# Two layers of gated cross-attention with feed-forward: batch 0's keys and queries copied to the stacks directly, queries stored once in rows of 1,600 bytes, scatters placed beside the value projection

## The reference

```python
# x: (16, 100, 256), ctx_1024: (16, 361, 256), mask: (16, 1, 100, 361)
q = split_heads(queries @ Wq + bq)
k = split_heads(keys @ Wk + bk)
v = split_heads(values @ Wv + bv)
scores = jnp.einsum('bhqd,bhkd->bhqk', q, k) / jnp.sqrt(jnp.float32(HD))
scores = jnp.where(mask, jnp.float32(-1000000000000000.0), scores)
attn = jax.nn.softmax(scores, axis=-1)
...
x = x + jnp.tanh(g_xattn[0]) * _L0_xattn_ref(_layernorm(x, axis=-1), ctx_1024, ctx_1024, mask, ...)
x = x + jnp.tanh(g_ffn[0]) * _L0_ffn_ref(_layernorm(x, axis=-1), ...)     # top 2 of 8 experts, and a shared one
x = x + jnp.tanh(g_xattn[1]) * _L1_xattn_ref(_layernorm(x, axis=-1), ctx_1024, ...)
x = x + jnp.tanh(g_ffn[1]) * _L1_ffn_ref(_layernorm(x, axis=-1), ...)     # top 1 of 8, low-rank additions
```

## Time and profile before

| | us |
|---|---|
| median of 3 runs | 911.53 |
| lowest and highest | 909.79, 912.62 |
| the profiled execution | 903.28 |
| its span | 901.4 |
| its mean granted TensorE clock | 0.951 |

### The profile page before, as it was taken

How to read it: one execution, slowest core, us unless ns; L and a number is a source line. 1 busy time by engine, 2 the same in 40 slices (tenths; PEclk the granted TensorE clock), 3 DMA queues, 4 the chain that set the end, 5 groups by cost and what they waited for, 6 DMA issues and landing times.

```text
span 901.4 us, 22259 instructions
## 1 busy us (share of the span) xinstructions
PE 794.3 (88%) x7992; PEld 614.1 (68%) x7992; DVE 582.5 (65%) x1773; ACT 471.0 (52%) x1004; POOL 221.3 (25%) x213
## 2 busy tenths in 40 slices
PE   5579999998999987899997689889999999778996
PEld 3346777766676665578985467667677676557996
DVE  4867778776666665675546478778788777463332
ACT  2335556555455545645663156556566565535453
POOL 2535222233332314410007253224212111000000
PEclk9789999999999999999999679999999999879999
DMA  6966778776676741733324958878898875000001
GB/s 186 236 155 163 165 148 176 160 156 139 144 164 148 164 107 34 216 94 107 123 86 112 180 127 173 198 186 176 189 192 161 181 159 97 2 1 1 19 19 37
DMA packets 152379, 119.00 MB, mean 132 GB/s; under 512 B 81020, under 2 KB 143848, under 8 KB 152264
## 3 DMA queue, kind: packets, MB, share of 16 engines
q1 hardware_dynamic: 146656, 109.91, 54.6%
q0 software_dynamic: 4096, 6.57, 2.8%
q10 hardware_dynamic: 1520, 1.12, 0.5%
HBM read 77.84 MB, written 39.46 MB: 130 GB/s over the span
## 4 chain that ended last, share of the span: by engine, by line
PE 61%; DMA 12%; DVE 10%; issue 7%; SPq 5%; ACT 3%; POOL 1%; DVEq 0%; ACTq 0%; POOLq 0%
PE ps L1895 18%; PE ps L2008 8%; PE ps L2034 7%; PE ps L2067 6%; PE ps L2057 5%; DMA cT<-in_ctxT 5%; PE ps L2053 3%; DMA QS<-mp 3%; DMA scr_q<-qp 2%; PE ps L2091 2%; PE ps L2322 2%; DMA QS<-scr_q 2%; DVE mx L1523 2%; DVE ps L1519 2%; SPq L409 1%
## 5 line engine op out<-in xcount | busy, mean ns | idle before, releaser
L965 ACT ACTIVATE prob<-ps 128x400 f32<-128x400 f32 (+1 forms) x384 | 182.6, 500 | 95.9 <-PE ps L2057 88.5
L2034 PE MATMUL ps<-KS,QS 96*100 96x361 bf16 x512 | 168.0, 344 | 24.4 <-DVE mx L1519 9.7
L1519 DVE CUSTOM_DVE_ANT_0 ps<-ps,biasq 100x361 f32<-100x361 f32 x256 | 135.7, 542 | 72.7 <-PE ps L2034 68.9
L1523 DVE TENSOR_REDUCE mx<-ps 100x1 f32<-100x361 f32 x256 | 127.1, 527 | 55.1 <-PE ps L2034 52.5
L2057 PEld LDWEIGHTS ps<-QS,KS 98*128 98x128 bf16 x1536 | 110.2, 101 | 50.8 <-issue 11.2
L2057 PE MATMUL ps<-QS,KS 98*128 98x100 bf16 x1536 | 134.8, 212 | 6.2 <-ACT prob L965 4.5
L2008 PE MATMUL ps<-cT,wk 128*128 128x361 f32 x256 | 103.0, 514 | 16.5 <-DMA ident<-in_ident 9.3
L2034 PEld LDWEIGHTS ps<-KS,QS 96*100 96x100 bf16 x512 | 65.1, 128 | 62.0 <-DVE mx L1519 16.2
L2067 PE MATMUL ps<-prob,V 128*17 128x100 f32 (+1 forms) x3072 | 88.4, 255 | 11.8 <-issue 11.8
L702 POOL TENSOR_TENSOR kp<-kr,kp 128x722 bf16<-128x722 f32 x32 | 48.5, 1517 | 187.2 <-ACT kp L936 187.0
L2067 PEld LDWEIGHTS ps<-prob,V 128*17 128x17 f32 (+1 forms) x3072 | 67.7, 99 | 29.7 <-issue 26.5
(11 more groups left out here) (226 smaller groups left out, 1621.1 us busy)
## 6 DMA issues: line engine op xcount, KB each, us to landing
scr_k<-kp SPq DMA_DIRECT2D x96, 180.5 KB, 5.1
KS<-scr_k SPq DMA_DIRECT2D x64, 270.8 KB
cT<-in_ctxT SPq DMA_DIRECT2D x32, 361.0 KB, 4.5
KS<-scr_k SPq DMA_DIRECT2D x64, 180.5 KB
QS<-scr_q SPq DMA_DIRECT2D x64, 150.0 KB
KS<-scr_k SPq DMA_DIRECT2D x64, 90.2 KB
scr_q<-qp SPq DMA_DIRECT2D x24, 200.0 KB, 3.6
scr_q<-qp SPq DMA_DIRECT2D x48, 100.0 KB, 5.1
```

Of the source, the lines that this page charges most:

```text
L965: nc.scalar.activation(prob[0:KROWS[t], t, hg, :], ps[0:KROWS[t], c % 2, 0:HQ * S], ACT.Exp).then_inc(a["exp"], 1)
L1519: nc.vector.tensor_tensor_reduce(ps[0:S, banks[h % len(banks)], 0:S2], ps[0:S, banks[h % len(banks)], 0:S2], biasq[p][:, :], 1.0, -3.0e38, ...
L1523: nc.vector.reduce_max(mx[:, h:h + 1], ps[0:S, banks[h % len(banks)], 0:S2], axis=AX.X).then_inc(a["max"], 1)
L2034: mm(ps[0:S, banks[h % len(banks)], 0:S2], QS[p][0:SROWS, h, :], KS[p][0:SROWS, h * S2:(h + 1) * S2], start=True, stop=True).then_inc(a["s ...
```

## The change

**Batch 0.** In both layers its keys and queries go from `kp` and `qp` straight into KS[0] and QS[0] by DMA, 12 copies of 16 partitions x 8 heads each for keys, 12 for queries, in halves. The two halves of queries have semaphores of their own. For this the columns of the projection weights are ordered by half, then dimension, then head. `k_first` of batch 1 now waits until batch 0's keys have been copied, and that of batch 2 until the stores of batch 1 have landed.

**Query stores and loads.** Each piece is stored once, in two halves, six DMAs in all. A load of half a batch is three DMAs, whose source is repeated by a zero stride where a piece is needed three times or twice; a row is 8 heads x 100 columns = 1,600 bytes.

**Scatters.** One for each of the steps n = 8 to 11, two for each of 12 to 15, twelve in all; they wait for `pv`, the end of the burst. Twenty follow behind the last burst: three, the norm of the last pair, five, the two low pieces, twelve.

**The rest.** The rows of ones come from a small memset through `scr_ones` in DRAM; the memsets of V stand at the program's start; SP loads the small vectors first; layer 1's last weights are loaded in steps 8 to 13 (before, 2 to 10); in both prologues TensorE, ScalarE, VectorE and GpSimd have another order, with the first maxima ahead of the norm that stood before them.

```diff
+        SCATTERS = {8: (0,), 9: (1,), 10: (2,), 11: (3,), 12: (4, 5), 13: (6, 7), 14: (8, 9), 15: (10, 11)}
...
+            def first_keys(l, part, halves):
...
+                for half in halves:
+                    c = slice(half * HH * S2, (half + 1) * HH * S2)
+                    for r in range(NST):
+                        if KPART[r] == part:
+                            sp.dma_start(KS[0][r * HD:(r + 1) * HD, c], kp[:, part, half, :]).then_inc(sd["kload"][half][0], 16)
+
+            def first_queries(l, half):
+
+                for r in range(NST):
+                    queries_split(l, 0, QPART[r])
+                    sp.dma_start(QS[0][r * HD:(r + 1) * HD, half * HH:(half + 1) * HH, :],
+                                 qp[0][:, QPART[r], half, 0:S]).then_inc(s_fq[half], 16)
...
-                sp.dma_start(QS[p][0:SROWS, hs, :],
-                             scr_q[:, :, :, bass.ds(n * S, S)].rearrange("j k (d h) n -> (j k d) h n", h=H)[:, hs]).then_inc(sd["kload"][half][p], 16)
+                for part, (r, copies) in enumerate(QRUNS):
+                    rows = scr_q[half, part, n].rearrange("(d h) n -> d (h n)", h=HH)
+                    sp.dma_start(QS[p][r * HD:(r + copies) * HD, half * HH:(half + 1) * HH, :],
+                                 bc(rows.unsqueeze(0), [copies, HD, HH * S])).then_inc(sd["kload"][half][p], 16)
...
-                for r in range(NST):
...
-                    sp.dma_start(scr_q[r, :, :, g * GT:(g + 1) * GT].rearrange("k p n -> p k n"),
-                                 qp[u][:, QPART[r], :, :]).then_inc(q["stored"], 16)
+                for part in range(NPIECE):
+                    queries_split(l, g, part)
+                    for half in range(KT):
+                        sp.dma_start(scr_q[half, part, g * nb + t0:(g + 1) * nb].rearrange("t p n -> p t n"),
+                                     qp[u][:, part, half, t0 * S:nb * S].rearrange("p (t n) -> p t n", n=S)).then_inc(q["stored"], 16)
...
-                    nc.gpsimd.memset(KS[1][SROWS:KSROWS, :], 1.0).then_inc(s_vones, 1)
...
                         if n >= 8:
-                            pool.wait_ge(sa[0]["sT"], START + 3 * NHG * (n - 1))
-                            scatter(n - 8)
+                            pool.wait_ge(sa[0]["pv"], START + NHG * n)
+                            for i in SCATTERS[n]:
+                                scatter(i // 2, i % 2)
...
+            for i in range(12, 15):
+                scatter(i // 2, i % 2)
             norm_pair(F0, NPAIR - 1)
...
+            for i in range(15, 20):
+                scatter(i // 2, i % 2)
             for j in POOL_PIECES:
                 low_piece(j)
+            for i in range(20, 2 * B):
+                scatter(i // 2, i % 2)
```

394 lines of the change are left out of this document (202 added, 192 removed).

## The result

The changed kernel takes 969.14 us (median of 4 runs, 960.96 to 978.24) against 912.08 for the kernel before in the same comparison. One of the four, the 978.24, was a slow execution, and the ratio leaves it out: 1.059, its 95% interval 1.050 to 1.068. The forecast was a gain of 2%. The range, 870 to 928, does not hold the time, and the sign is wrong. The profiled run of the changed kernel took 971.69 us, its span 969.8, with a mean granted clock of 0.914 in place of 0.951.

What follows compares the result with a forecast made beforehand. TensorE, busy for 88% of the span, was taken as the limit, savings lying in its pauses, lowered clock and slower instructions. Terms -18 - 5 + 7 - 10 - 7 + 4 + 10 = -19: 884 us profiled, 892 median, range 870 to 928.

Steps and rivals of the forecast that it cites:

- steady steps: query stores and loads: Steps of both layers: more load issues in SP's queue, less a saved wait; +4 in layer 0, +10 in layer 1.
- The 3.9 us taken off for smaller stores: Layer 1's steps: halved query store bytes can remove the 3.9 us wait for the query stack.
- rival B: Steps of both layers: query loads fill two or three DMA engines and slow every step; 937 us, chance 0.19.
- Prologue of layer 0: Start of layer 0: direct copies give earlier scores, and VectorE's pause of 6.46 us goes; -10 us, bounds -6 and -13.
- Prologue of layer 1: Start of layer 1: direct copies take away the 4.28 us wait for the query stack; -7 us (-3 to -11).
- Rival C: Both prologues: they don't shorten, batch 1's stack arriving late, and give 3 of 17 us; 906 us, chance 0.10.
- Scatters: Layer 0's steps: scatters moved behind the burst no longer stall TensorE; -18 us, bounds -20 and -7.
- rival A: Layer 0's steps: scatters behind the burst hold ScalarE, then TensorE, so stalls move; 901 us, chance 0.15.
- Behind step 14: Layer 0 after step 14: four scatters issued later no longer hold ScalarE's copy and TensorE; -5 us (-3 to -6).
- The later slot rows: After layer 0's steps: last scatters come later, slot rows turn 6.5 us late, TensorE restarts below its clock; +7 (0 to +9).
- The wait that I named as its mark: Before the slot rows are turned: a wait of about 5 us would show the price of later scatters.

Runs made afterwards that it cites:

- The rung for them: Changed kernel with the query stores and loads of before, each half's load in three DMAs, source not repeated: 908.02 us, ratio 1.033.
- the first comparison: Here: kernel before with only the scatters moved, twelve in the steps after the burst, twenty behind them: 887.17 us, 0.987 against the kernel before at 898.12.
- the third: Here: kernel before with its scatters in the same pairs, each pair and the last twelve waiting for the burst's end: 894.54 us, ratio 0.998.
- The ladder: Changed kernel with old query traffic 892.12 us; plus three loads per half 908.02; plus repeated source in 200-byte runs 1035.48; plus each piece stored once 1015.36.

## Why the prediction was wrong

**The term "steady steps: query stores and loads" failed.** It had +14 us with bounds of -4 and +40. With the old traffic put back, layer 0's and layer 1's periods are 14 and 26 us shorter, 41 in all, just above the upper bound. 12 more come back ahead of the first burst and 4 between the layers, where the prediction charged nothing to the query traffic.

The issues were not the mistake. I had priced four more a step, 1.8 us of SP's queue, at +4 in layer 0 and +14 in layer 1. The rung for them measured 16 us in all, 6.4 and 13.9 by the periods, and the same edit on the kernel before 14. The price came out right, though SP's queue was taken for a side road: that its slack lies in layer 0 and in the odd steps, and is near nothing in most even steps of layer 1, was not looked up.

Two other steps were wrong. The 3.9 us taken off for smaller stores did not come off: TensorE's wait for the query stack in layer 1 is 20.9 us. And the loads from a repeated source had no price in the sum. They stood in rival B alone. What is left of the 57 us when the 16 for the issues are taken off, 41 us, belongs to them and to the new stores together.

Rival B had the premise, and at 937 the right side, with a chance of 0.19. It was priced as throughput: how much busy time 106 KB are on two engines, and whether that fits into a step. I held it for less likely on the argument that an average rate understates two engines working alone. The runs show a price in another place. The mean share of the DMA engines is 0.61, yet the maxima land 1.1 us later in layer 0's median step and 0.7 in layer 1's, and from the last query store's issue to the query load behind it in the shown step it is 6.7 us for 5.1. The maxima's landing stands in SP's queue in each step, the query stores' in every second step of layer 1. A later landing in such a queue costs, however low the mean share. The runs show that the landings are later, not on which engines.

**Prologue of layer 0: -10 forecast, +10 in the changed kernel.** The maxima are ready 3.3 us earlier (57.10 for 60.39), then step 0 waits. Queues of SP, ScalarE and TensorE, 57 to 77 us:

```profile
57.47 5.84 SPq L472 DMA_DIRECT2D scr_q<-qp  x6
...
67.93 8.35 SPq L472 DMA_DIRECT2D scr_q<-qp  x6
73.14 1.08 ACT L930 ACTIVATE qp<-ps,bq 128x400 bf16<-128x400 f32 x2 [14.40 <-DMA scr_q<-qp]
...
75.12 2.00 PE L2295 MATMUL ps<-wo,onT 128*100 128x256 f32 x4 [14.21 <-issue]
...
76.91 0.81 PE L2071 MATMUL ps<-KS,QS 96*100 96x361 bf16 x2
```

The stores of group 1 are issued at 57.47, where they were issued at 37.17 before; ScalarE waits 14.40 us until they have landed before it may write group 3's queries, and step 0 starts at 76.91, not at 66.52. I read the prologue along TensorE's and VectorE's waits only, and didn't follow the store that was moved behind batch 1's loads. The question to ask of it was who waits for its buffer. With the old traffic put back, the first burst starts at 75.9 us, and the kernel of the same comparison that has the old prologue has it at 78.7: 3 us of the 10 are real. The scores begin at 33.77 us as forecast (33.5), though a direct copy takes 0.63 us to issue (six in 3.80) and not 0.45. The pause of 6.46 us did not go whole: TensorE waits 1.94 us for the context at 37.70 and 3.34 us for VectorE's maxima at 43.33.

**Prologue of layer 1: -7 forecast, nothing found.** TensorE's wait for the query stack of 4.28 us became one of 4.80 in the kernel with the old traffic and 6.37 in the changed one: the 24 direct copies are issued in 16.4 us, and the queries' stand at the end of each half. From the last burst of layer 0 to the first of layer 1 it is 186.5 us with the old traffic and the new prologue, and 186.0 with the scatters alone and the old prologue: no gain. Rival C had this outcome. Its reason, a late stack of batch 1, is another; here it is batch 0's that isn't earlier.

**Scatters: -18 forecast; what they gave is open.** The burst is in one piece, in a step with a scatter behind it:

```profile
210.13 1.75 PE L2104 MATMUL ps<-prob,V 128*17 128x100 f32 x72
```

That looks like the forecast come true, and the difference of the traces, -12.4, has its sign. But the kernel before with three query loads has its bursts in one piece too, with the pairs where they were. So the step from "these steps have a pair of scatters" to "the pair stalls them" was not sound: the stall belongs to that execution and something beside the pair, and the eight steps can be 17.2 to 18.2 us long without moving a scatter. What is measured is the whole edit: 11 us, against 16 forecast, in the first comparison; and nothing for pairs behind the burst in the third. What stayed in the steps with two scatters is not rival A's hold-up of ScalarE, whose copy of the burst's result starts 0.8 us after the burst there, but the late key piece and VectorE's slow operation.

**Behind step 14: -5 forecast.** The traces give -4.8, from 17.3 to 12.5 us, but the 12.5 stand also in the kernel with three query loads and the scatters unmoved. The agreement is luck, or at least no proof.

**The later slot rows: +7 forecast, +7.5 by the traces** with the scatters alone. In the changed kernel the last scatter and the turn of the first slot rows answer to the earlier trace rows:

```profile
406.27 0.99 POOL L849 DMA_INDIRECT scr_x<-xn,posi  x1 [0.30 <-issue]
...
411.73 0.41 PE L2350 MATMUL ps<-ident,xg 128*128 128x128 f32 x2 [0.17 <-DMA xg<-scr_x]
```

From the last burst's start to the turn it is 40.8 us (370.94 to 411.73) where it was 35.0, so 5.8 late against the 6.5 forecast. The wait that I named as its mark isn't there: 0.17 us. What the stretch has more of is TensorE's slower clock (0.92 for 0.95) and two pauses of 1.5 us for "issue" in the shared expert's work. The size was right, the sign that I gave for it was not.

## What to carry to other kernels

Where one queue issues nearly all DMAs and waits in it for landings, walk it round one whole step, odd and even, before costing an edit, and write down its slack; where it has none, issues and later landings are paid, even if another engine is busy for 88%. A stall that stands beside an instruction in one trace is not yet caused by it: before a gain is built on it, look for the same pair in a second trace. A load that repeats a source by a zero stride in its outermost dimension is to be compared with the same load without it before it is built on, with short runs above all. Stored bytes that are saved are worth nothing if they are paid in DMAs or in landings in that queue. Of the kernels run here, the kernel before with the scatters alone moved has the lowest ratio, 0.987 (0.982 to 0.992); as ratios move by 2% between comparisons, it can't be ranked against the 0.992 and 0.993 with the old query traffic.

## What had not been expected of the hardware

- The same three loads took 1.88 us of SP's issuing, and 5.05 us when two of them had a repeated source in runs of 200 bytes; in rows of 1,600 bytes 1.84.
- The kernel's time rose by 14% from this repeated source alone, while the number of DMAs and of bytes moved was the same.
- A VectorE operation on 100 x 16 numbers took 0.17 us in the kernel before, and 2.0 us or more in six of six places behind a pair of scatters, beside an elementwise operation of GpSimd.
- The same pair of scatters beside a burst of 72 small matmuls went with a burst of 3.9 us in one trace and of 1.8 us in another.

Open: how the 57 us are divided in the changed kernel itself. The ladder measures the issues at 16 us and the repeated source at 127, but the latter with short rows. What it costs with rows of 1,600 bytes is left as the difference, some 40 us, taken across two comparisons, in which the new stores are contained; no run has these rows and stores, no repeated source and the same number of DMAs, since a DMA for each copy adds issues. Why a repeated source holds up the issuing, and what besides the scatters broke the bursts of the kernel before, isn't shown either.
